# Expert sums taken onto the residual by accumulating transfers instead of loads and GpSimd additions

## The reference, cut to what matters

```python
xn = _layernorm(x)
x = x + _L0_attn_ref(xn, ...) + _L0_ffn_ref(xn, ...)    # layer 0
xn = _layernorm(x)
x = x + _L1_attn_ref(xn, ...) + _L1_ffn_ref(xn, ...)    # layer 1
```

## Time and profile before

| | |
|---|---|
| median of 3 runs | 1380.31 us (1378.53 to 1382.48) |
| profiled execution, its own time | 1380.49 us |
| its span, first to last instruction | 1378.4 us |
| PE, DVE, ACT, POOL busy | 92%, 49%, 38%, 51% of the span |
| layer 0 ends (last addition of DVE) | 422.87 us |

### The profile page before, as it was taken

How to read it: one execution, slowest core, us unless ns; L and a number is a source line. 1 busy time by engine, 2 the same in 40 slices (tenths; PEclk the granted TensorE clock), 3 DMA queues, 4 the chain that set the end, 5 groups by cost and what they waited for, 6 DMA issues and landing times. The chain is left out here.

```text
span 1378.4 us, 20455 instructions
## 1 busy us (share of the span) xinstructions
PE 1274.4 (92%) x7267; PEld 1028.0 (75%) x7267; DVE 672.1 (49%) x1363; ACT 520.5 (38%) x1124; POOL 700.2 (51%) x553
## 2 busy tenths in 40 slices
PE   4488899999977999999999999999999977999998
PEld 3366588888865887888788888888888863666655
DVE  4699555554577557555654335433443331222223
ACT  2344466566664433334333343333433321111110
POOL 3333487878663465677765656655565440000014
PEclk9789999999997999999999999999999997999999
DMA  6800188888652411111221111111111109311113
GB/s 225 283 1 1 45 174 182 181 182 180 126 161 82 127 59 50 58 61 54 71 76 54 51 51 61 50 51 62 50 35 35 35 0 353 116 46 47 56 50 113
DMA packets 97987, 127.38 MB, mean 92 GB/s; under 512 B 11744, under 2 KB 81248, under 8 KB 97760
## 3 DMA queue, kind: packets, MB, share of 16 engines
q1 hardware_dynamic: 82912, 99.85, 22.8%
q0 software_dynamic: 14976, 26.23, 9.5%
HBM read 97.83 MB, written 28.21 MB: 91 GB/s over the span
## 5 line engine op out<-in xcount | busy, mean ns | idle before, releaser
L1517 PE MATMUL a_p_p<-a_xr,a_wr 128*128 128x512 f32 x1152 | 308.7, 403 | 2.4 <-DVE g_x L2062 2.4
L1517 PEld LDWEIGHTS a_p_p<-a_xr,a_wr 128*128 128x128 f32 x1152 | 206.6, 189 | 42.6 <-DVE g_x L2062 3.1
L1836 POOL TENSOR_TENSOR a_sqsum<-a_sqsum,a_sq 128x512 f32<-128x512 f32 x60 | 77.9, 1298 | 228.1 <-ACT a_sq L1720 228.1
L1802 POOL TENSOR_TENSOR a_wr<-g_hold,a_wr 128x768 fp32r<-128x768 f32 x64 | 124.2, 1940 | 17.4 <-DVE a_wr L1868 17.4
L1901 DVE SCALAR_TENSOR_TENSOR a_gated<-a_th,a_p_o 128x512 f32<-128x512 f32 x64 | 44.0, 688 | 159.2 <-ACT a_sq L1720 159.2
L408 POOL DMA_INDIRECT acc<-l_ye,g_slot_token x64 | 104.8, 1637 | 32.8 <-issue 16.5
L1154 POOL DMA_DIRECT2D out<-e_ye x24 | 13.1, 547 | 193.8 <-DVE e_ye L1304 193.8
L1838 POOL TENSOR_TENSOR a_gr<-a_gated,a_gr 128x512 fp32r<-128x512 f32 x64 | 97.9, 1529 | 23.7 <-DVE a_gr L1905 23.7
L1530 PE MATMUL a_p_p<-a_wvr,a_xr 128*128 128x512 f32 x384 | 105.2, 410 | 0.3 <-DVE a_xr L1862 0.3
L1588 PE MATMUL a_p_w<-a_gr,l_wo_r 128*128 128x512 f32 x384 | 100.7, 397 | 2.3 <-POOL a_gr L1838 2.3
L1881 DVE TENSOR_TENSOR a_sc<-a_p_s,g_hold 128x512 f32<-128x512 f32 x64 | 44.1, 690 | 103.2 <-PE a_p_s L1546 102.8
(11 more groups left out here) (267 smaller groups left out, 2766.3 us busy)
## 6 DMA issues: line engine op xcount, KB each, us to landing
g_hold<-in_Wqkg SPq DMA_DIRECT2D x64, 384.0 KB, 3.2
g_hold<-in_gate_up SPq DMA_DIRECT2D x64, 192.0 KB, 3.0
g_hold<-in_Wv SPq DMA_DIRECT2D x16, 512.0 KB, 4.6
e_up<-in_gate_up SPq DMA_DIRECT2D x8, 1024.0 KB, 13.6
l_down<-in_down SPq DMA_DIRECT2D x64, 96.0 KB, 3.6
acc<-l_zero SPq DMA_DIRECT2D x2, 2176.0 KB, 11.7
l_lists<-acc SPq DMA_DIRECT2D x8, 512.0 KB, 4.9
e_down<-in_down SPq DMA_DIRECT2D x8, 512.0 KB, 12.3
```

The lines of the kernel that those rows point to most:

```text
L1517: mm = pe.matmul(dst[:, :], wr[n % 2][:, wp, kk, c * P:(c + 1) * P], xr[n // H1 % 2][:, xp, kk, :], start=(kk, xp, wp) == (0, 0, 0), stop= ...
L1802: pool.tensor_tensor(wr[n % 2][:, 1, :, :], w[n % 2], wr[n % 2][:, 0, :, :], ALU.subtract).then_inc(w_parts, 1)
L1836: pool.tensor_tensor(sqsum[b % 2][:, :], sqsum[b % 2][:, :], sq[a % 2][:, :], ALU.add).then_inc(summed, 1)
```

## The change

The eight loads and POOL's additions are gone. POOL itself now waits for `summed` and issues accumulating transfers that add rows of `acc[0]` and then of `acc[1]` onto `x` in SBUF, 512 rows (4 tiles) in each for chunks 0 to 2. The second transfer of a chunk waits until the first has landed (`part_in[c]`), since both change the same bytes. Chunk 3 is cut in two: tiles 12 to 14 are added in the same way (384 rows each), after `added` has reached 15 (tile 14); tile 15 is loaded by SP from both tables into `late`, and DVE adds these two at step 61, ahead of tile 15's `add_out`. The statistics wait for `part_in[c]` to reach 32 and, for tiles 12 to 14, move from step 66 to step 68, ahead of `add_out(15)`.

```diff
@@ SP
-            def parts(c):
-                if c >= 2:
-                    sp.wait_ge(combined, c - 1)
-                for i in range(2):
-                    acc = g["acc"][i][c * SEQ:(c + 1) * SEQ, :].rearrange("(t p) d -> p t d", p=P)
-                    sp.dma_start(part[c % 2][i], acc).then_inc(part_in[c], 16)
...
-            for c in range(TPB):
-                parts(c)
+            for i in range(2):
+                sp.dma_start(late[i], g["acc"][i][(NT - 1) * P:NT * P, :]).then_inc(late_in, 16)
@@ POOL
+            for s in range(YR):
+                pool.wait_ge(summed[s], 16 * (E0 // YR))
             pool.wait_ge(biased, NT)
+
+            def accumulate(c, i, tiles):
+                if i:
+                    pool.wait_ge(part_in[c], 16)
+                acc = g["acc"][i][tiles.start * P:tiles.stop * P, :].rearrange("(t p) d -> p t d", p=P)
+                pool.dma_start(g["x"][:, tiles.start:tiles.stop, :], acc, accum_op=ALU.add).then_inc(part_in[c], 16)
+
             pool.wait_ge(added, 3 * TPB)
-            for c in range(TPB):
-                at = slice(TPB * c, TPB * (c + 1))
-                pool.wait_ge(part_in[c], 32)
-                pool.tensor_tensor(part[c % 2][0], part[c % 2][0], part[c % 2][1], ALU.add).then_inc(joined, 1)
-                if c < TPB - 1:
-                    pool.wait_ge(joined, c + 1)
-                    pool.tensor_tensor(g["x"][:, at, :], g["x"][:, at, :], part[c % 2][0], ALU.add).then_inc(combined, 1)
+            for i in range(2):
+                for c in range(TPB - 1):
+                    accumulate(c, i, range(TPB * c, TPB * (c + 1)))
+            pool.wait_ge(added, NT - 1)
+            for i in range(2):
+                accumulate(TPB - 1, i, range(NT - TPB, NT - 1))
             pool.wait_ge(decays_done, 1)
@@ DVE
             def statistics1(c, tiles):
-                if c < TPB - 1:
-                    dve.wait_ge(combined, c + 1)
+                dve.wait_ge(part_in[c], 32)
...
-            def combine_last():
-                at = slice(NT - TPB, NT)
-                dve.wait_ge(joined, TPB)
-                dve.wait_ge(added, NT - 1)
-                dve.tensor_tensor(g["x"][:, at, :], g["x"][:, at, :], part[(TPB - 1) % 2][0], ALU.add).then_inc(combined, 1)
-                dve.wait_ge(combined, TPB)
-                statistics1(TPB - 1, range(NT - TPB, NT - 1))
...
+                if n == STATS1[0]:
+                    dve.wait_ge(late_in, 32)
+                    dve.wait_ge(biased, NT)
+                    for i in range(2):
+                        dve.tensor_tensor(g["x"][:, NT - 1, :], g["x"][:, NT - 1, :], late[i], ALU.add).then_inc(joined, 1)
+                        dve.wait_ge(joined, i + 1)
                 if n in STATS1:
                     c = STATS1.index(n)
                     statistics1(c, range(TPB * c, TPB * (c + 1)))
-                if n == LAST - 8:
-                    combine_last()
+                if n == LAST - 6:
+                    statistics1(TPB - 1, range(NT - TPB, NT - 1))
```

More of the change, by code:

```diff
@@ L181, in layer0 @@
         queue = lists[:, 3, :].rearrange("p (t n) -> p t n", t=NT // 2)
-        part = [[lists[:, 2 * s + i, :].rearrange("p (t d) -> p t d", t=TPB) for i in range(2)] for s in range(2)]
+        late = [lists[:, i, 0:D] for i in range(2)]
         stats1 = m.sb("stats1", [P, NT - 1, 6])
@@ L246, in layer0 @@
                  "ex_in_psum", "exT_ready", "h_in_psum", "th_ready", "silu_ready", "hT_ready", "ye_in_psum", "ye_ready",
-                 "slopes_in", "slope_ready", "decays_done", "causal_done", "next_in", "joined", "combined", "stats1_done", "var1_ready",
+                 "slopes_in", "slope_ready", "decays_done", "causal_done", "next_in", "late_in", "joined", "stats1_done", "var1_ready",
                  "std1_ready", "rstd1_ready")
@@ L257, in layer0 @@
          ex_in_psum, exT_ready, h_in_psum, th_ready, silu_ready, hT_ready, ye_in_psum, ye_ready,
-         slopes_in, slope_ready, decays_done, causal_done, next_in, joined, combined, stats1_done, var1_ready,
+         slopes_in, slope_ready, decays_done, causal_done, next_in, late_in, joined, stats1_done, var1_ready,
          std1_ready, rstd1_ready) = (m.sem(n) for n in names)
```

## The result

| | kernel before | changed kernel |
|---|---|---|
| median of 20 runs each | 1381.13 us (1378.53 to 1386.19) | 1384.99 us (1381.01 to 1390.04) |
| ratio | | 1.0023, 95% interval 1.0013 to 1.0034 |
| span of the profiled execution | 1378.4 us | 1383.5 us |

The ratio says 0.23%, some 3.2 us, and the two medians lie 3.9 us apart: the change costs more than nothing, and less than the 0.3% that the forecast took as the bound of "no change".

What follows compares the result with a forecast made beforehand. PE, busy 92% of the span, bounds the kernel, so only work it waits for counts. Layer 0 ending at 429.1 instead of 422.87 adds 6.2 us: 1380.49 becomes 1386.7, less 0.18 for the median: 1386.5 us; range 1375 to 1396.

Steps and rivals of the forecast that it cites:

- two reads a packet: Rival: accumulating transfers take twice a plain packet's time, 0.102 us; layer 0 ends at 421.0, total 1378.4 us; chance 0.25.
- The price of a packet, 0.130 us: Accumulating transfers: each 1 KB packet takes 0.130 us on a DMA engine, so 4.2 us for 512 rows, 3.1 for 384.
- the lone scatter: Accumulating scatter in the trace before: 144 packets, 9 per engine, in 1.17 us; source of the 0.130 us packet price.
- the first rival: Same as "two reads a packet": 0.102 us a packet, 1.2 us stall at step 61, 1378.4 us; chance 0.25.
- The stall of 4.9 us at step 61: DVE, ready at 398.65, waits for chunk 0, seen at 403.55, before its statistics: 4.9 us.
- the 416.0: Forecast moment of tile 14's addition: 408.0 plus 4.9 of stall, plus 3.1 for PE's lowered clock.
- the part of the working that had no stall: DVE up to tile 14: if nothing else waited, work is 2.0 us earlier and tile 14 added at 408.0, not 412.57.
- The pair behind tile 14: Two serial accumulating transfers for tiles 12 to 14: 5.35 us each plus 0.3 between, landed at 427.0.
- the 0.75: Each accumulating transfer: 0.55 us for the start after issuing plus 0.2 us for the semaphore at the end.
- as fast as a plain transfer: Rival: accumulating packets take 0.051 us, issuing 1.1 us; the pair behind tile 14 takes 6.4 us, total 1373.9 us; chance 0.17.
- The mask multiplication, costed at nothing: POOL's 4.52 us mask multiplication after the last issue, 423.1 to 427.6, was taken as hidden before layer 0's end at 429.1.
- the forecast's 6.2 us more for layer 0's end: End of tile 15's addition on DVE at 429.1 against 422.87 before: 6.2 us more.

Runs made afterwards that it cites:

- e11: Changed kernel with plain transfers in place of the eight accumulating ones, so additions onto tiles 0 to 14 are left out: 1380.49 us, one run, no ratio.
- e9: Changed kernel with the mask multiplication moved from POOL to DVE, in quarters at steps 64 and 66: 1386.45 us, ratio 1.0013 to the kernel before.
- e3: Changed kernel with chunk 3 summed early in a buffer and added by DVE after tile 14: 1386.42 us, ratio 1.0014 to the kernel before.
- e1: Changed kernel run again, no edit: 1387.65 us, ratio 1.0029 to the kernel before.
- e8: Changed kernel, no edit, for a third trace: 1383.63 us, one run, only the trace is read.
- e5: Changed kernel with POOL's mask multiplication moved into the next block, still on POOL: 1391.05 us, ratio 1.0075 to the kernel before.
- e10: Changed kernel with e6's transfers (chunk 3 early) and e9's mask multiplication on DVE: 1378.97 us, ratio 0.9962 to the kernel before.
- e7: Kernel before, no edit, for a second trace: 1385.11 us, one run, only the trace is read.
- e12: The kernel of e10 run once more: 1377.55 us, ratio 0.9958 to the kernel before.
- e4: Kernel before with one wait more, so POOL's mask multiplication waits for tile 14's addition: 1384.2 us, ratio 1.0005 to the kernel before.
- e6: Changed kernel with e3 and e5 together, chunks ordered 0, 1, 0, 2, 1, 2, DVE's addition one step later: 1384.71 us, ratio 1.0024.

## Why the prediction was right in its time and wrong in its course

The forecast was 1386.5 us, 6.0 over the profiled execution; measured were 1384.99, a ratio of 1.0023, well inside the range of 1375 to 1396. Most weight was on slower by over 0.3% (0.49); what came was the 0.31 for a time within it. The course that was to lead there did not happen in its first half, and that the time came out near is luck. In the profiled execution of the changed kernel, against the forecast of 1386.7 for it, layer 0 ended 8.2 us earlier (420.9 for 429.1). Against the trace of before, which the forecast took over from there on, the start of the next block then cost 1.1 us more (2.8 for 1.7), the way to the first square sum 4.6 us more (41.5 for 36.9, the second fall of the clock), and the rest 1.3 us more. That sums to 1.2 us less than forecast.

The rival "two reads a packet" had the course: a wait of 1.2 us at step 61 (0.77), tile 14 at 409.2 (407.9) and layer 0's end at 421.0 (420.9). Its time, 1378.4 us, was 6.6 us too low because neither it nor the forecast counted what comes behind layer 0's end.

1. **The price of a packet, 0.130 us: the step that failed.** Taken from the lone scatter, whose target is memory. Measured are 0.104 us of own time and, since they overlap, 0.083 us a packet in passing. That is the first rival's price (0.102), a little bettered: 197 GB/s is 0.53 of the 369 GB/s of plain transfers in e11. The lone scatter's price did not carry over to an accumulation in SBUF; whether for its target or because it was alone, no run shows. The Trainium skill, page "Collectives: The Full Stack", section on the bandwidth ceiling, gives a reduction between cores half the rate of a copy, since it reads two sources. The 0.53 agrees with that; that the second read is the cause here was not tested.
2. **The stall of 4.9 us at step 61** was 0.77 us (0.77 to 1.49 over the traces of the changed kernel and e9). The first rival had 1.2. With the stall went PE's gap and the fall of the clock ahead of tile 14, hence the 416.0: tile 14 was added at 407.94, against 408.0 in the part of the working that had no stall. That part (2.67 - 0.9 + 0.25 = 2.0 us, L954 and L985 back to 0.43 and 0.17) was right in each term; that the sum hit 407.94 so closely is again two things that offset each other, the last scatter 0.9 us earlier in this execution and the wait of 0.77 us. e3 shows that the course itself was possible: there a wait of 2.67 us and a stalled L984 did open the gap, and the clock fell; in e9 a short fall came behind a wait of 1.49 us and a gap of 2.08 us on PE.
3. **The pair behind tile 14.** Forecast 11.0 us, measured 10.87; the sum right, its terms not: issuing 1.28 instead of 1.5 us, moving 384 KB 2.0 us instead of 3.1 (393 KB at 197 GB/s), and start and end together 5.41 - 1.28 - 2.0 = 2.1 us instead of 0.75. The first plain transfer of e11's pair gives the same 2.1 us (3.90 - 0.75 - 1.06), the second 1.8. So 1.35 us too little for start and end stood against 1.1 us too much for moving and 0.2 too much for issuing, in each of the two transfers. The first two had both been taken from the lone scatter, the 0.75 as what was left of its best landing. The rival "as fast as a plain transfer", 6.4 us for the pair, was wrong in size too by the same term: plain transfers need 7.5, and 3.6 to 3.9 us for one of 384 KB instead of its 3.05.
4. **The mask multiplication, costed at nothing: the step that was missed.** The working compared its end with DVE's last operation. But the block ends for POOL only with the DRAIN behind it, 2.9 us later in the changed kernel, e1, e8 and e11 (3.9 us before, where 7 us of cover remained). 419.46 + 2.9 = 422.4 is 1.2 us behind DVE. The three traces of the changed kernel have 2.8 to 3.1 us between the last addition and the next block, the two of before 1.7. e5 and e9, without it there, have 1.7. POOL's DRAIN also waits for POOL's transfers: where no multiplication followed, it ended 1.6 us after the last landing (e5, e9, e10), which in e5 and e9 is 0.5 us ahead of DVE.
5. **The sum.** Tile 14 is 3.4 us earlier (31.8 against 35.2); the pair with the statistics then takes 13.0 us in place of 8.0 (full clock) or 10.3 (low clock), on average 3.9 more; POOL's DRAIN adds 1.3. On average over the traces the next block starts 47.8 us after the last scatter, against 46.0: **+1.8 us**. The first square sum is at 87.0 against 85.2, +1.8 too, and the rest of the 3.2 us is not settled: from the last scatter to the end the traces have 1005.1 against 1002.8 us on average, but with three and two traces and a clock that alone moves 4 us from one execution to the next these means are no better than about 2 us.

Counted from the last scatter, the forecast's 6.2 us more for layer 0's end were thus 1.0 us less against the trace it was built on (44.5 against 45.5), or 1.3 more against the trace with a full clock; the profiled span was 5.1 us longer all the same, because the clock fell a second time at 448 us. A comparison of these two profiles alone would have put it down to the change; e7 and e8 show that it isn't.

## What to carry to other kernels

A transfer that accumulates is no free addition: it took about twice a plain one's time to move, and 2 us to start and report (a plain one too). It cost where it sat in series behind the last producer (the pair of the changed kernel). Run early into a buffer of its own, with one quick addition by DVE late, it was part of the one kernel that gained (e10, e12), whose share for each edit is open. Cost the instructions with which an engine leaves a block, not only its last visible one. And where GpSimd works beside DVE in a chain that sets the end, look at what it stalls: moving the multiplication (e3, e4, e5, e6) moved the stall, and where it stalled nothing (the changed kernel) its DRAIN ended the block. Taken off GpSimd (e9, e10) it did neither. When a time comes out as forecast, compare the moments on the way as well: here a rival had all of them and the forecast had the time.

## What the runs showed of the hardware that was not expected

- Accumulating transfers were cut into packets of 1 KB where plain ones of the same pattern on the same queue were not (3412 for 3.4 MB, 1232 for 4.06 MB), and the packets' times overlapped (a DMA share of 1.24).
- Issuing an accumulating transfer took 1.28 to 1.34 us for 512 and for 384 rows alike, a plain one 0.75 to 0.80; DVE operations beside it kept their times (L971 0.42 and L1046 0.44 each beside the issue at 396.04).
- POOL's DRAIN at the end of a block ended 2.9 us after the mask multiplication in the changed kernel (e11 too), 3.8 to 3.9 in before, e7 and e4, and about 1.6 us after the landing of the last accumulating transfer where that came later (e3, e5, e9, e10). Why 2.9 here and 3.9 there is open.
- The same kernel loses its clock in one execution and keeps it in the next at the same place (450 to 458 us at 0.50 in two of five traces of the two kernels), which costs 4 us, more than the change.
